# Seven pairs of units in a recurrent mixer: a sequence written out in full becomes a loop on every engine

## The reference

```
h    = rmsnorm(x) * norm_w
proj = h @ in_proj_w.T                      # gate | hid, B, C | dt
hBC  = silu(causal_conv(hBC, conv_w, conv_b))  # 4 taps along the sequence
A_cs = cumsum(A * dt)                       # within chunks of 128
M      = (C B^T) * exp(segsum(A))           # per head
Y_diag = M @ (hid*dt)                       # inside a chunk
states = B^T (decay * hid*dt)               # one state per chunk, carried on
Y_off  = (C @ carried_state) * exp(A_cs)
y   = (Y_diag + Y_off + D*hid) * silu(gate)
out = x + rmsnorm_per_group(y) * gnorm_w @ out_proj_w.T
```

## Time and profile before

| | |
|---|---|
| median of 3 runs | 2091.21 us (2091.2 to 2091.69) |
| the profiled execution | 2091.69 us |
| its span, first to last instruction | 2089.7 us |
| PE busy | 1991.2 us (95%), granted clock 0.983 |
| DVE, ACT, POOL busy | 75%, 70%, 57% |
| the seven pairs of units in the middle of the mixer | 643.99 to 2010.08 us of the span, 1366.09 us |

### The profile page before, as it was taken

One profiled execution on the slowest core, in us unless ns is written; L12 is line 12 of the kernel. 1 busy time (PEld: TensorE's weight loads), 2 busy tenths in 40 slices (PEclk: granted clock), 3 DMA queues, 4 the chain that ended last, 5 costly groups with the idle time before them and its releaser, 6 DMA issues.

```text
span 2089.7 us, 32789 instructions
## 1 busy us (share of the span) xinstructions
PE 1991.2 (95%) x10930; PEld 1595.1 (76%) x10930; DVE 1575.5 (75%) x2963; ACT 1469.3 (70%) x2933; POOL 1198.6 (57%) x823
## 2 busy tenths in 40 slices
PE   6999698989899999999999999999999999999986
PEld 5564466667688888888888888888888888888875
DVE  4546787875678787878788777888787878778776
ACT  3142675644778788878778777878787888778774
POOL 2514455663466556566666656666666566566655
PEclk9999799999999999999999999999999999999998
DMA  7404323243233333333342433343333333333433
GB/s 279 121 21 126 101 72 115 92 141 126 88 128 124 115 114 115 119 112 112 114 126 89 135 106 127 102 132 121 101 115 127 114 111 115 104 127 104 135 110 115
DMA packets 113798, 243.04 MB, mean 116 GB/s; under 512 B 23648, under 2 KB 24672, under 8 KB 112736
## 3 DMA queue, kind: packets, MB, share of 16 engines
q1 hardware_dynamic: 109792, 228.37, 33.6%
q0 software_dynamic: 3840, 12.59, 2.0%
HBM read 228.06 MB, written 12.85 MB: 115 GB/s over the span
## 4 chain that ended last, share of the span: by engine, by line
PE 74%; DVE 1%; issue 1%; ACT 1%; DMA 0%; SPq 0%; DVEq 0%; ACTq 0%
PE s_ps L71 13%; PE s_ps L73 13%; PE s_ps L72 13%; PE s_ps L1548 6%; PE s_ps_o L73 5%; PE s_ps_o L71 5%; PE s_ps_o L72 5%; PE s_ps L1518 5%; PE s_ps L1556 4%; PE s_ps L1510 3%; PE s_ps L1538 1%; PE s_ps L1496 1%; ACT s_lm L1628 0%; DMA s_wo_raw<-in_w_out 0%; PE s_ps L1502 0%
## 5 line engine op out<-in xcount | busy, mean ns | idle before, releaser
L1930 POOL TENSOR_TENSOR w_lo<-w_raw,w_hi 128x1024 fp32r<-128x1024 f32 x142 | 340.0, 2399 | 550.0 <-ACT w_hi L1610 550.0
L71 PE MATMUL s_ps<-h_hi,w_hi 128*128 128x512 f32 x1152 | 464.4, 403 | 8.9 <-DVE s_hid L1779 5.8
L73 PE MATMUL s_ps<-h_hi,w_lo 128*128 128x512 f32 x1152 | 451.6, 392 | 0.0
L72 PE MATMUL s_ps<-h_lo,w_hi 128*128 128x512 f32 x1152 | 450.2, 391 | 0.0
L1774 DVE SCALAR_TENSOR_TENSOR s_cv<-s_ps,s_par,s_cv 128x511 f32<-128x511 f32 (+2 forms) x480 | 355.9, 744 | 19.5 <-ACT s_cv L1653 13.7
L1947 POOL TENSOR_TENSOR s_lm<-s_lm,s_cbt 128x512 f32<-128x512 f32 x256 | 326.1, 1296 | 12.5 <-ACT s_lm L1635 12.5
L1628 ACT ACTIVATE s_lm<-s_rows,s_steps 128x128 f32<-128x128 f32 x1024 | 312.5, 390 | 2.2 <-PE s_ps L1548 2.2
L1653 ACT ACTIVATE s_cv<-s_ps,s_par 128x512 f32<-128x512 f32 x160 | 124.7, 779 | 228.4 <-PE s_ps L73 228.4
L71 PEld LDWEIGHTS s_ps<-h_hi,w_hi 128*128 128x128 f32 x1152 | 217.3, 189 | 55.5 <-DVE s_hid L1779 6.7
L73 PEld LDWEIGHTS s_ps<-h_hi,w_lo 128*128 128x128 f32 x1152 | 217.2, 189 | 47.8
L72 PEld LDWEIGHTS s_ps<-h_lo,w_hi 128*128 128x128 f32 x1152 | 217.8, 189 | 41.4
(11 more groups left out here) (232 smaller groups left out, 4087.1 us busy)
## 6 DMA issues: line engine op xcount, KB each, us to landing
w_raw<-in_w_in SPq DMA_DIRECT2D x144, 512.0 KB, 3.5
s_rows<-acs_dram SPq DMA_DIRECT2D x256, 256.0 KB, 4.4
s_wo_raw<-in_w_out SPq DMA_DIRECT2D x128, 256.0 KB, 3.4
w_raw<-in_gu_q SPq DMA_DIRECT2D x14, 512.0 KB, 3.5
f_d_q<-in_d_q SPq DMA_DIRECT2D x28, 256.0 KB, 2.6
f_d_w<-in_d_s SPq DMA_DIRECT2D x28, 256.0 KB, 3.4
table<-xn SPq DMA_DIRECT2D x16, 256.0 KB, 8.5
xs<-in_x SPq DMA_DIRECT2D x8, 256.0 KB, 4.7
```

The costliest lines, as they stand in the source:

```text
L71: nc.tensor.matmul(dst, l_hi, r_hi, start=start, stop=False)
L72: nc.tensor.matmul(dst, l_hi, r_lo, start=False, stop=False)
L73: return nc.tensor.matmul(dst, l_lo, r_hi, start=False, stop=stop)
L1930: nc.gpsimd.tensor_tensor(w_lo[:, slot, :], w_raw[:, slot, :], w_hi[:, slot, :].bitcast(F32), ALU.subtract).then_inc(w_lo_ready, 1)
```

## The change

In `schedule` the Python loop over g, which wrote 7 pairs of units into the program one after the other, becomes a loop of the engine's own (`eng.Fori`). g is then a register.

```
@@ -1975,7 +1975,7 @@

             unit(eng, Unit(-1, 1))
             unit(eng, Unit(0, 0, first=True))
-            for g in range(GROUPS - 1):
+            with eng.Fori(0, GROUPS - 1) as g:
                 unit(eng, Unit(g, 1))
                 unit(eng, Unit(g + 1, 0))
             unit(eng, Unit(GROUPS - 1, 1, last=True))
```

## The result

| | before | after |
|---|---|---|
| runs beside each other, us, median (range) | 2091.45 (2091.20 to 2091.69), 4 runs | 2103.97 (2102.55 to 2104.58), 4 runs |
| ratio to before | | 1.0059 (95%: 1.0041 to 1.0077) |
| profiled execution / its span, us | 2091.69 / 2089.7 | 2100.83 / 2098.8 |
| the seven pairs (112 slots), us | 1366.09 | 1379.41 |

The loop costs 12.5 us, 0.6%. The forecast was 28 us: right in sign, more than twice too large.

A forecast was written before the change was run, and what follows sets the result against it. PE, released by DVE at T without slack, was taken as the bound; 22.4 us in the slots plus 5.6 us for the ways back made 28 us, 2120 us in all, with an 8-in-10 range of 2096 to 2160 us.

The forecast's parts named there:

- What bounds it: Seven pairs: PE busy throughout, 1366.09 us, released by DVE at T; any PE wait lengthens the run, 112 times.
- (A): T on PE: a register instruction carries the bank wait, so T's weight load starts later; 0.10 us a slot.
- (B): OFF's scaling on DVE: a register instruction carries the wait, so DVE's chain begins later; 0.10 us a slot.
- (C): Between T and G, PE's sequencer has two register instructions and a wait instead of one wait; 0.05 us a slot.
- The slack of this release is thus used up: T's load on PE, 0.11 us late: DVE's chain from OFF to second carry (4.3 us) matches PE's work meanwhile.
- the 0.10 for its own waits: Slot 0 of each unit: its own waits ahead of the small products add 0.10 us.
- (D): Ways back at pass ends: branch and possible instruction fetch, 0.8 us each, seven times, 5.6 us; upper bound 3.5 each.
- (E): SP: a register instruction and a wait more for nearly every load, reaching nobody; costs nothing.
- 1 (ways back decide): At the ways back all engines lose their lead and fetch repeatedly, about 5 us each; 57 us, 2149; chance 0.15.
- 2 (sequencers): PE's sequencer becomes the bound: 108 register instructions a pass at 0.1 us, uncovered; 76 us, 2168; chance 0.08.
- 3 (register instructions run ahead): Register instructions at T and OFF run ahead, load within 0.07 us of the carry; not slower, 2092 to 2094; chance 0.11.

The follow-up runs named there:

- e8: Changed kernel with the second wait's value computed ahead of both waits and a closing-branch hint on every engine; seven pairs 1366.11 us, run 2094.39 us, ratio 1.0015.
- e1: Changed kernel with a hint on every engine naming the loop's closing branch; seven pairs 1371.67 us, run 2099.97 us, ratio 1.0049.
- e2: Changed kernel with two waits reordered, for T on PE and OFF's scaling on DVE; seven pairs 1375.70 us, run 2101.91 us, ratio 1.0054.
- e7: Changed kernel, no hint, with the second wait's value computed into a register ahead of both waits; seven pairs 1374.14 us, run 2099.14 us, ratio 1.0046.
- e4: Changed kernel with only PE looped, the other engines' pairs written out; seven pairs 1373.23 us, run 2095.55 us, ratio 1.0027.
- e6: Unrolled kernel before the change with two waits reordered, T's on PE and OFF's scaling on DVE; seven pairs 1370.40 us, run 2093.48 us, ratio 1.0013.
- e11: Changed kernel with the second wait's value computed ahead and the hint on all engines but SP; seven pairs 1366.35 us, run 2121.19 us, ratio 1.0001.

## Why the prediction was wrong in size

By its own steps:

- **What bounds it**: right. PE, released by DVE at T, pays per slot; in the loop PE's busy row stays and its idle places are those named.
- **(A)** 0.10 us forecast, 0.07 measured (0.053 to 0.123). **(B)** 0.10 forecast, 0.088 measured (0.313 to 0.401). **(C)** 0.05 forecast, 0 measured (e8). T's load came 0.16 us later, where A and B made 0.20.
- **"The slack of this release is thus used up": the step that failed.** I saw T's load 0.11 us late and its first matmul in step, and took this as the edge. It was not: the four loads of T stood 0.05 us wider than they had to, and with what the next matmuls make up PE could take another 0.07 to 0.08 us (table above). So a slot pays 0.16 - 0.08 = 0.08, not 0.25, and the ordinary slots cost 5.6 us (e1 against before), not 22.4. That T's first matmul stood 0.11 us behind its own load, which I had seen, is no second slack: in the kernel after it starts 0.01 us behind, and G's is late by 0.10 all the same.
- In which slots: 1, 3, 4, 7 as said, 5 not, 6 not (forecast 0.05). Slot 0 0.07 instead of 0.25: there A counts in full, and C and the 0.10 for its own waits are nothing. Slot 2 nothing, though T's load is as late there; I had put it with slot 1 and overlooked its later wait for DVE's `s_cT`.
- **(D)** right as a mechanism, too small as a term: 5.6 forecast, 7.7 measured. There are six ways back, not seven, at 1.3 us each (5.8 and 8.1 us in all in e2 and e7). I priced a single fetch by a load of 16 KB at 2.0 us; DVE and ACT stand for 3.2 to 4.2 us, PE for 4.4 to 4.6 with one packet in its branch, of which the packet itself is 1 us, and for 5.0 to 5.4 with two. PE's lead was 3.7 us, not some 3, and the branch less this lead is the loss. No pass lost more than 1.9 us, so each was under the upper bound of 3.5.
- The rule of the Trainium skill (Advanced Engine Details and Errata, ISA Cache: two lines of 256 instructions) agrees with the trace on four engines: PE and ACT (528) don't fit and fetch, POOL (165) and SP (302) don't fetch. DVE, with 495, fits by number, against what the prediction says of it, and still fetches; why stays open. The Trainium skill's 108 ns for a compare-and-branch (Advanced Engine Details and Errata, Control Flow Timing) is above the branch's own record on ACT, DVE, POOL and SP, 40 to 69 ns, and below what a taken one cost on POOL and SP up to the next instruction, 0.26 to 0.34 us; it tells nothing of the 4 us that count.
- **(E)** nothing, and nothing was seen in the stretch: e8's leaves no room for it.
- **Rivals.** 1 (ways back decide): half right. They are the larger part, 7.7 of 13.3, but at 1.3 us, not 5. 2 (sequencers): refuted by e8. 3 (register instructions run ahead) fails by its own sign: T's load 0.12 us behind the carry, slots at 11.31.

The two errors had opposite signs: 17 us too much in the slots, since a slack was counted as none, and 2 us too little in the ways back. The range of 8 in 10, 2096 to 2160 us, holds the result only because its lower end was drawn from small terms, not because a slack was seen.

## What to carry to other kernels

A late weight load is no proof that the slack is gone: look at the loads behind it, whether they already follow each other as closely as they can (0.39 us for four here) or can still close up, and price only what is over that. The distance of the first matmul from its own load says nothing more. In a loop on the sequencers, keep the signal that comes last on the engine's own instruction: write its wait first and compute the other wait's value ahead of both. Ask for the closing branch to be hinted on the engines that the trace shows standing for microseconds behind it; on SP, which went on after 0.3 us, the hint only cost 2 us at the end. With the held values and the hint, the seven pairs here ran as fast as unrolled code.

## What the runs showed of the hardware

- A taken back edge over 495 and 528 instructions cost DVE and ACT 3.2 to 4.2 us until the next instruction (after), and over PE's pass its branch took 3.7 to 5.4 us (24 of them in after, e2, e4 and e7); with a hint 0.36 to 0.50 on DVE and ACT (e1), and on PE 0.34 to 0.40 us in seven of twelve, 2.4 to 3.6 in the others (e1, e8). Over 165 and 302 instructions, on POOL and SP, it was 0.22 to 0.29 us without a hint.
- Packets of the instruction queues are 16 KB on PE's and 8 KB on the one of the other engines.
- A plain register instruction (ALU_OP) is 32 ns on PE and POOL, 35 on ACT, 37 on SP, 40 on DVE, the longer kind at the loop's head (FUSED_REGOPS) 68 to 90 ns, and an engine's instruction starts 0.084 us after the start of a plain one that a signal released (PE's weight load and DVE's scaling alike). Some 600 of them a pass cost no time where they don't carry the last signal (e8: 37059 instructions in the trace, 32789 before, over 7 passes).
- A wait in front of an instruction, instead of on it, makes it start 0.06 us later on PE and 0.07 us on DVE (e6 against before).
- The hint on SP, one instruction a pass, moved the end of the program by 2 us (e8 against e11).
